# Routing the second expert layer in two halves of four token tiles, with every sigmoid written as a tanh

## What is computed

```python
x = x + L0_attn(cond(x, f, f, w, u, t))
x = x + L0_ffn(cond2(x, ...))     # 16 experts, top 4, and a shared expert
x = x + L1_attn(cond(x, ...))     # 32 heads over 8 kv heads, causal
x = x + L1_ffn(cond2(x, ...))     # 8 experts, top 2

# cond: a factor that doesn't depend on x, times a sigmoid of x
base = sigmoid(r) * (num / maximum(den, 1e-08))
out = base * (0.8 + 0.2 * tf)
# L1_ffn
gate_weights = softmax(x @ Wg + bg); topv, topi = top_k(gate_weights, 2)
h = gelu(x @ W1 + b1); h = gelu(h @ W2 + b2); eo = h @ W3 + b3
out = sum over the two chosen experts of eo * topv
```

## Time and profile before

| | |
|---|---|
| median of 3 runs | 1190.07 us |
| lowest, highest | 1188.19, 1195.08 us |
| the profiled execution | 1180.62 us, span 1178.8 us |
| mean granted TensorE clock, profiled | 0.946 |
| busy: PE, DVE, ACT, POOL | 990.3, 800.5, 603.1, 210.7 us |

### The profile page before, as it was taken

The page is one execution under the profiler, slowest core; times in us unless marked ns, Lnnn a source line. Parts: engine busy times, 40 slices in busy tenths (PEclk is TensorE's granted clock), DMA queues, the critical chain, the costliest instruction groups (busy, mean ns, idle before and its releaser), DMA issues.

```text
span 1178.8 us, 18449 instructions
## 1 busy us (share of the span) xinstructions
PE 990.3 (84%) x6324; PEld 705.0 (60%) x6324; DVE 800.5 (68%) x2057; ACT 603.1 (51%) x1457; POOL 210.7 (18%) x175
## 2 busy tenths in 40 slices
PE   1889888987989799598988888789889867998895
PEld 1767666766777677463655656433333345887784
DVE  6588887888788978764388885666767451554442
ACT  3398638854884488422433332256647613454442
POOL 1001010111011001127233334000000050222323
PEclk9999999999999999889999999789999856999998
DMA  9999600000000000124588985135455346676772
GB/s 262 239 228 229 153 1 1 2 1 1 1 1 1 1 2 1 47 83 164 159 277 270 288 274 181 73 143 215 175 182 214 144 142 221 184 243 194 224 227 27
DMA packets 75277, 161.30 MB, mean 137 GB/s; under 512 B 10658, under 2 KB 57262, under 8 KB 70960
## 3 DMA queue, kind: packets, MB, share of 16 engines
q1 hardware_dynamic: 66304, 145.52, 40.6%
q0 software_dynamic: 8880, 14.60, 4.8%
HBM read 127.68 MB, written 62.62 MB: 161 GB/s over the span
## 4 chain that ended last, share of the span: by engine, by line
PE 47%; DVE 18%; DMA 15%; ACT 8%; issue 6%; POOL 3%; SPq 1%; ACTq 0%; POOLq 0%; DVEq 0%
PE ps L1607 43%; DMA out<-arena 8%; DMA arena<-in_w0all 3%; DMA made<-arena 3%; DVE arena L1405 2%; POOL out L515 2%; DVE arena L1094 2%; DVE arena L1070 1%; POOL slots L504 1%; ACT arena L616 1%; DVE den L940 1%; DVE arena L1032 1%; ACT arena L601 1%; ACT arena L609 1%; ACT arena L594 1%
## 5 line engine op out<-in xcount | busy, mean ns | idle before, releaser
L1607 PE MATMUL ps<-arena 128*128 128x256 f16 (+15 forms) x4712 | 773.9, 340 | 68.1 <-ACT arena L609 19.6
L1607 PEld LDWEIGHTS ps<-arena 128*128 128x128 f32 (+8 forms) x4712 | 527.7, 148 | 239.9 <-issue 107.4
L1591 DVE CAST arena<-arena 128x256 f16<-128x256 f32 x120 | 36.9, 307 | 107.9 <-ACT arena L819 106.8
L1405 DVE TENSOR_REDUCE arena<-ps 128x4 f16<-128x1024 f32 (+1 forms) x48 | 58.8, 1227 | 50.0 <-PE ps L1607 50.0
L819 ACT ACTIVATE arena<-ps,arena 128x256 f32<-128x256 f32 x120 | 55.6, 474 | 59.5 <-PE ps L1607 56.8
L1094 DVE SCALAR_TENSOR_TENSOR arena<-arena 128x128 f32<-128x128 f32 x240 | 84.0, 411 | 0.7 <-issue 0.3
L452 POOL TENSOR_TENSOR den<-den,backd 128x512 f32<-128x512 f32 x8 | 10.2, 1270 | 398.9 <-DVE euv L921 398.9
L616 ACT ACTIVATE arena<-ident,arena 128x128 f32<-128x128 f32 x256 | 81.0, 391 | 0.0
L515 POOL DMA_INDIRECT out<-arena x30 | 47.1, 1572 | 149.9 <-DMA out<-arena 86.1
L731 ACT ACTIVATE arena<-ps 128x1024 f32<-128x1024 f32 x48 | 49.2, 1025 | 44.8 <-PE ps L1607 44.7
L484 POOL DMA_INDIRECT made<-arena x47 | 53.1, 1129 | 105.6 <-DVE arena L1318 103.7
(11 more groups left out here) (291 smaller groups left out, 1284.3 us busy)
## 6 DMA issues: line engine op xcount, KB each, us to landing
arena<-split SPq DMA_DIRECT2D x15, 2048.0 KB
arena<-in_w0all SPq DMA_DIRECT2D x47, 608.0 KB
slots<-in_blank SPq DMA_DIRECT2D x17, 1040.0 KB, 16.6
arena<-in_w1all SPq DMA_DIRECT2D x16, 1024.0 KB, 6.6
split<-arena SPq DMA_DIRECT2D x32, 512.0 KB, 3.8
slots<-in_blank SPq DMA_DIRECT2D x9, 1072.0 KB, 19.3
arena<-slots SPq DMA_DIRECT2D x47, 130.0 KB
side<-made SPq DMA_DIRECT2D x8, 512.0 KB, 5.8
```

The costliest lines, as they stand in the source:

```text
L1405: dve.tensor_reduce(out, ps[:, at:at + 2].rearrange("p j (r s) -> p j r s", r=nr), X, ALU.max, negate=True).then_inc(max1_done, 1)
L1607: return pe.matmul(o, l, r, start=start, stop=stop, skip_group_check=shared)
```

## The change

`HEAD` becomes `TAU // 2`: the first stage of the routing takes four tiles (batches 0 and 1), the second the other four. All of the first stage is written into steps 6 and 7 of the attention; the sigmoid, the conditioning and the logits of batch 2 are a piece of their own, and so are those of batch 3, but their choice of experts and their scatters are made together. In the second stage `place_rows` stands ahead of the table. The base is cut in two on PE: `base_rows` (turned `xT`) and `base_bias` (`b3`), and the first half of both stands ahead of the route of batch 3. Every sigmoid becomes `tanh(x / 2)`, and the multiplication behind it `(t + 1) * factor`, the half being put into the factor.

```diff
-HEAD = TAU - TT
+HEAD = TAU // 2
+        def rows_bank(q):
+            return (7, 6, 4, 5)[q]
...
-                act.activation(hT[:, :, cols], xT[:, :, cols], ACT.Sigmoid).then_inc(route_act, 1)
+                act.activation(hT[:, :, cols], xT[:, :, cols], ACT.Tanh, scale=0.5).then_inc(route_act, 1)
...
-            cs(dve.tensor_scalar(oscale[:], small[:, 4:8], 0.2, 0.8, ALU.mult, ALU.add))
+            cs(dve.tensor_scalar(oscale[:], small[:, 4:8], 0.05, 0.45, ALU.mult, ALU.add))
...
-                st.tell(dve.tensor_tensor(hT[:, :, cols], hT[:, :, cols], fac[:, which, :, cols], ALU.mult), h_ready, done)
+                st.tell(dve.scalar_tensor_tensor(hT[:, :, cols], hT[:, :, cols], 1.0, fac[:, which, :, cols], ALU.add, ALU.mult),
+                        h_ready, done)
...
# ACT, steps 6 and 7
-                if i + 2 == 2 * B:
-                    sigmoid_rows(slice(0, HEAD * P), B - 1)
+                    if i == 2 * B - 2 and k == 1:
+                        sigmoid_rows(slice(0, HEAD * P), 2)
+                    if i == 2 * B - 2 and k == 4:
+                        high_rows(0)
+                    if i == 2 * B - 1 and k == 0:
+                        exp_rows(slice(0, HEAD), 4)
+                        high_rows(1)
+                    if i == 2 * B - 1 and k == 1:
+                        sigmoid_rows(slice(HEAD * P, (HEAD + TT) * P), B - 1)
...
# DVE behind step 7
-            logits1(first, 2, 3)
-            normalise(2 * B - 1)
-            shares(pr1[:, first], mx1[:, first], 5)
-            choose1(first)
-            low_rows(0)
-            residual1(B - 1)
-            sum_tiles(first, 1)
-            condition_rows(3, slice(HEAD * P, NT), 6, 3)
-            combine(first, 1)
-            low_rows(1)
-            low_rows(2)
-            place_rows(first, 3, 1)
-            logits1(last, 4, 4)
+            place_rows(first, 3, 1)
+            normalise(2 * B - 1)
+            turned_combination(0)
+            low_rows(2)
+            residual1(B - 1)
+            condition_rows(3, slice((HEAD + TT) * P, NT), 7, 4)
+            logits1(last, 0, 5, 5)
...
# PE, steps 6 and 7
+                    if i == 2 * B - 2 and k == 3:
+                        pe.wait_ge(ld["moe1"], 7 * 16)
+                        route(wg1, E1, 2, range(HEAD), 6)
+                        pe.wait_ge(x_done, 2 * B - 1)
+                        turn_rows(0)
+                    if i == 2 * B - 2 and k == 5:
+                        pe.wait_ge(route_dve, 4)
+                        turn_rows(1)
...
-                else:
-                    pe.wait_ge(ld["moe1"], 7 * 16)
-                    route(wg1, E1, 2, range(HEAD))
...
+            def base_rows(q):
                 for half in range(2):
+                    tok = slice((2 * q + half) * P, (2 * q + half + 1) * P)
                     for k in range(CT):
+                        mm(ps[:, 2 + q, half * C + k * P:half * C + (k + 1) * P], xT[:, k, tok], ident[:],
+                           half + k == 0, False, True)
+
+            def base_bias(q):
+                for half in range(2):
+                    tok = slice((2 * q + half) * P, (2 * q + half + 1) * P)
+                    ins = mm(ps[:, 2 + q, half * C:(half + 1) * C], combT[0:E1, tok], b3[0:E1], False, half == 1, True)
+                ins.then_inc(base_pe, 1)
```

More of the change, by code:

```diff
@@ L528, in _ @@
             act.wait_ge(c_dve, 1)
-            act.activation(small[:, 4:8], small[:, 0:4], ACT.Sigmoid).then_inc(c_act, 1)
+            act.activation(small[:, 4:8], small[:, 0:4], ACT.Tanh, scale=0.5).then_inc(c_act, 1)
             act.wait_ge(c_dve, 2)
@@ L968, in condition_batch @@
                 dve.wait_ge(sig_ready, count)
[L969 removed]
+                st.tell(dve.scalar_tensor_tensor(xc[:], sig[:], 1.0, fac[:, which, :, bass.ds(b * T, T)], ALU.add, ALU.mult),
                         xc_ready, count)
@@ L1216, in _ @@
             shares(pr0, mx0, 2)
+            dve.wait_ge(route_act, 3)
+            st.tell(dve.tensor_scalar(sg0, sg0, 0.5, 0.5, ALU.mult, ALU.add), route_dve, 3)
             choose(pr0, top0, idf0, range(TAU))
@@ L1548, in _ @@
             combine(last, 2)
-            dve.wait_ge(route_pe, 5)
+            low_rows(3)
+            place_rows(last, 6, 2)
             count = ps[:, 1, TAU * E1:(TAU + 1) * E1]
@@ L2051, in project_out, with turn_rows, ranks1 @@
                 ins.then_inc(wo1_pe, 1)
+            def turn_rows(q):
+                for half in range(2):
+                    for k in range(CT):
+                        tau = 2 * q + half
+                        ins = pe.transpose(ps[:, rows_bank(q), half * C + k * P:half * C + (k + 1) * P],
+                                           hT[:, k, tau * P:(tau + 1) * P], ident[:])
+                ins.then_inc(turned_h, 1)
+            def ranks1(part, told):
+                pe.wait_ge(sel_ready, told)
+                ranks = ps[:, 1, part.start * E1:part.stop * E1]
+                mm(ranks, before_after[:, 0], sel1[:, part].rearrange("p a e -> p (a e)"), True, False, True)
+                ins = mm(ranks, before_after[:, 1], sums1[:, part].rearrange("p a e -> p (a e)"), False, True, True)
+                if part.stop == TAU:
+                    ins = mm(ps[:, 1, TAU * E1:(TAU + 1) * E1], before_after[:, 1], sums1[:, TAU], True, True, True)
+                ins.then_inc(route_pe, 1)
             results_turned(0)
@@ L2107, in _ @@
+            def base_bias(q):
+                for half in range(2):
+                    tok = slice((2 * q + half) * P, (2 * q + half + 1) * P)
+                    ins = mm(ps[:, 2 + q, half * C:(half + 1) * C], combT[0:E1, tok], b3[0:E1], False, half == 1, True)
+                ins.then_inc(base_pe, 1)
+            ranks1(slice(0, HEAD), 1)
             turn_outputs(2 * B - 1)
-            turn_rows(0)
+            route(wg1, E1, 3, range(HEAD, HEAD + TT))
+            turn_combination(0)
@@ L2109, in _ @@
             turn_o(B - 1)
-            turn_rows(1)
+            turn_rows(2)
             project_out(B - 1)
-            turn_rows(2)
-            ranks1(slice(0, HEAD), 1)
-            route(wg1, E1, 3, range(HEAD, TAU))
+            base_rows(0)
+            base_rows(1)
+            pe.wait_ge(combT_ready, 1)
+            base_bias(0)
+            base_bias(1)
+            route(wg1, E1, 4, range(HEAD + TT, TAU))
             turn_rows(3)
+            pe.wait_ge(low_ready, 3)
+            base_rows(2)
@@ L2134, in turn_tile @@
+            pe.wait_ge(low_ready, 4)
+            base_rows(3)
+            pe.wait_ge(combT_ready, 2)
+            base_bias(2)
+            base_bias(3)
             def turn_tile(j):
```

171 lines of the change are left out of this document (80 added, 91 removed).

## The result

The kernel became faster by 0.6 to 0.7%, a little more than forecast.

The account below looks back on a forecast made before the run. No engine was taken to bound the whole, each stage having its own limit. First expert matmul 980.9 for 987.2, plus 0.4 for fused multiplication, gave -5.9: 1184.2 us from 1190.07, range 1182 to 1186, 8 in 10 from 1179 to 1190.5.

Parts of the forecast that it names:

- The turn: Attention step 6 to 7: read-out at 916.1 not 917.76 (-1.7), second table load gone (-1.3), together -3.0 us.
- Step 6: Attention step 6, PE without a gap: a route of four tiles and two `turn_rows` add 2.8 us (1.0 to 4.0).
- Step 7: Attention step 7: PE piece at full clock -2.0 us, ACT's added exponentials, read-out and sigmoid +1.2.
- the clock term: Step 7: PE's 7.05 us piece at full instead of half clock behind a shorter hole, -2.0 us (0 to -3.5).
- Clock 1.00 through step 7: Sign that the prediction is right: the profile shows PE's granted clock at 1.00 throughout attention step 7.
- The last read-out: End of the attention: the route of six tiles goes from ahead of the last values, -2.8 us.
- Behind it: After the attention: slot numbers at 955.7 not 961.80, last scatter -6.3 us, first expert matmul at 980.9.
- Slower: Rival: the base block ahead of batch 3's route delays everything behind it; 1196 us, chance 0.09.
- Same: Rival: base block (+3.7) or step 7 (+2.0) at half clock leaves -2 to -4 us, no measurable change; chance 0.19.
- The drain: Rival: each table switch holds ACT 1.38 us longer, so three on the path give 4.1 more, 1180 us; chance 0.02.
- Rows behind weights: Rival: first tiles' rows wait for 4 MB of weights until 976; decides only if the table comes after 961; no chance given.
- The gain is larger: Rival: the last scatter lands in 4 us, not 7.96, winning 3 us more, -9 in all; chance 0.20.

Follow-up runs that it names:

- before_again: The kernel before once more, unaltered, for a second profiled execution; one timed run, 1189.97 us.
- after_again: The changed kernel once more, unaltered, for a second profile; 1178.98 us, 0.993 of before.
- after_third: The changed kernel unaltered a third time, timed on one chip with two further-edited kernels; 1170.37 us, 0.9929 of before.
- group A: The runs whose median of before, timed beside them, was 1188 to 1190 us; the chip number doesn't tell the groups apart.
- group B: The runs whose median of before, timed beside them, was 1179 to 1180 us.
- before_places_first: The kernel before with the last two tiles' slot numbers computed ahead of the tile table; 0.9979 of before.
- three parts: The changed kernel with batch 2 selected and placed in its own part: 0.9906 of before; with table first 0.9914, with base last as well 0.9901.

## Why the prediction came out as it did

**The turn** (-3.0): -2.8 and -2.9 measured, step (6,5) to step (7,0). The two loads are worth what they last and little more. That the activation of 1.48 us left the turn too brought only 0.1 us more (4.6 for 4.7 with tanh alone), since the read-out then waits for PE. The Trainium skill, "ScalarE: Activation LUTs", section "What ACT_TABLE_LOAD costs", adds some 1.38 us of drain to each; 2.8 us for two speaks against that here.

**Step 6** (+2.8): +2.2 in two profiles of the changed kernel and +3.7 in the third, where the clock falls, within the bounds of 1.0 and 4.0.

**Step 7** (-2.0, +1.2): from 12.1 us (11.8 in before_again) to 10.6 and 11.8. Tanh alone gives 9.7, so the clock term is 2.4 us, and the additions are worth +0.9; a fall of the clock adds 1.2 where it comes. "Clock 1.00 through step 7" holds in only half of the profiles. The windows of after_again:

```profile
923.00:924.00 1.00, 1.00 (x8) 0.14 (x4) 0.75 (x1) 1.00 (x2) 0.00 (x0) 0.62 0.26 98
924.00:925.00 1.00, 1.00 (x5) 0.08 (x2) 1.00 (x3) 0.63 (x2) 0.00 (x0) 0.50 0.00 0
...
931.00:932.00 1.00, 0.16 (x2) 0.00 (x0) 0.00 (x0) 1.00 (x2) 0.00 (x0) 1.00 1.02 406
932.00:933.00 1.00, 0.71 (x6) 0.28 (x8) 0.22 (x1) 1.00 (x4) 0.00 (x0) 1.00 1.15 279
...
934.00:935.00 1.00, 1.00 (x4) 0.13 (x2) 0.65 (x5) 1.00 (x3) 0.00 (x0) 0.50 0.96 385
```

Twice, 10 us apart, the granted clock is 0.50 for some 3 us, with PE busy in each of these windows. Ahead of the first fall PE had been busy for 15 us; ahead of the second it had waited 1.12 us at the turn. The same wait of 1.12 us stands in the profiles without a fall. The two falls make 2.7 of the 3.9 us between exponentials of 166.6 and of 170.5 us. The other 1.2 lie ahead of step 6, where the profiles differ in the same way: at the turn from step 4 to step 5 after_again has a granted clock of 0.52 over 7 us, and after_third has 1.00. Of the eight profiles with tanh and early routing four have the two falls.

**The last read-out** (route of six tiles gone, -2.8): 4.8 us behind the last exponentials before, 2.2 after, -2.6. The attention in all: -5.4 or -1.5 us, as the clock falls or not (168.8 or 172.7 for 174.2); -3.8 had been forecast. Of the -5.4, 0.7 us were won in steps 0 to 5 (134.7 for 135.4), ahead of the places that the forecast priced.

**Behind it.** Offsets from the last read-out, us:

| | before | forecast | after, A | after_third, B |
|---|---|---|---|---|
| projection ended | 7.4 | 8.0 | 6.5 | 6.5 |
| last logits on DVE | 13.9 | 14.8 | 14.0 | 11.3 |
| slot numbers | 23.9 | 21.6 | 20.9 | 18.1 |
| last scatter | 33.9 | 31.3 | 30.1 | 27.3 |
| first expert matmul | 49.3 | 46.8 | 44.7 | 42.7 |

This is the mis-sized part: -2.5 forecast, -4.6 measured in group A and -5.5 in group B (42.65 for the 48.11 of before_places_first). Two terms did it. The projection came 1.5 us earlier than charged, as the turns ahead of it run at full clock: `turn_outputs` takes 1.09 us for 1.97. And the base block was charged 5.5 us, "nearer to full clock", where its bound of 4.6 was already too high: at full clock it takes 3.9. In group A an unnamed wait of 2.7 us gave that back at the logits. From the logits on the forecast's increments are right: 6.8 us to the numbers (6.9 in both), 9.7 to the last scatter (9.2), 15.5 to the expert matmul (14.6 and 15.4).

**The rivals.** "Slower" rested on the base block ahead of batch 3's route: it was the wrong place to look. With the block ahead of the route the clock stays at 1.00 there, and moved between route and ranks it costs 4.6 us. "Same" did not come; half clock for the block was seen only where it was moved. "The drain" is refuted by the turn. "Rows behind weights" did not decide in the changed kernel, and may have in the one with three parts. "The gain is larger" came half true, though not by its mechanism: the last scatter's rows still took 7.13 us to land (7.96 before).

**The size.** -5.9 us forecast for the stretch; -10.0, -6.0 and, in group B against before_places_first, -11.0 measured. The medians differ by 8.7 to 8.9 us, and the ratios say 7.1 to 8.4. So the forecast was somewhat too small, and that it came close is partly luck: its sum has no fall of the clock inside steps 6 and 7, which takes back 2.7 us in half of the profiles, and this made up for a stretch behind the attention that was priced too high. From the first expert matmul to the end the profiles spread from 186.1 to 194.8 us with no order by kernel (191.6 before, 188.4 after), as the forecast said of a stretch that the change doesn't touch.

## What to carry to other kernels

When work is moved into a busy step, price all that it brings along: with sigmoids the early routing put four switches of table into steps 6 and 7, and its times show no gain. Before a block is moved off a critical route, look what clock it will run at and what is queued behind it. This block took 3.9 us at 1.00 and 7.5 at 0.50; that cost 4.6 us where the last ranks were queued behind it, and nothing where they were not. When one engine is freed, ask whether another was late already: DVE was, in the kernels with three parts. And compare from a milestone near the change: two profiles of one kernel began the stage 11 us apart, more than the whole gain.

## What the runs showed of the hardware

The granted clock can fall to 0.50 without a hole just ahead of it. In four of eight profiles it did so in step 6, after PE had been busy in every window of 1 us from 908 to 923 (after_again). In the same four it fell again 10 us later, just behind a wait of PE of 1.12 us, which the other four have too, without a fall. What decides between the two is not shown.

In group A something held PE or its signal for 2.6 to 9.3 us beyond a unit's 3.4 in the first layer. In the kernels with the early routing it did so for 2.7 us ahead of the last logits as well; the profile gives the wait to "remote". Both places lie beside POOL's scatters, and in the kernels before, whose scatters begin only behind the last logits, the second wait is missing. In group B neither shows, though the scatters are the same, and before ran in 1178.8 to 1180.3 us there, for 1187.7 and 1189.7 in group A. What is held, and what makes the groups, stays open: no run here could separate the two.
